# VectorE's order in an embedding tower on one Trainium2 core: the bias of a column step ahead of the scaling of the step before

## The reference, cut to what matters

```
x = layer_norm(dense_t @ Wd.T, gd, bd)
y = layer_norm(jnp.einsum('bnd,ed->bne', sparse_t, Ws), gs, bs)
y = jnp.einsum('bne,pn->bep', y, Wsi)
y = layer_norm(y, gsi, bsi)
y = jnp.swapaxes(y, 1, 2)
T = jnp.concatenate([x[:, None, :], y], axis=1)
Z = jnp.einsum('bnd,bmd->bnm', T, T)
out = layer_norm(Z[:, TRIL_I, TRIL_J] @ Wl.T, gl, bl)
h = jnp.concatenate([out * mask, r_dense_t], axis=1)
h = jnp.maximum(h @ W_top1 + b_top1, 0.0)
h = jnp.maximum(h @ W_top2 + b_top2, 0.0)
y = h @ W_top3
```

## Time and profile before

| what | value |
|---|---|
| runs of the kernel | 614.75, 616.3, 616.88 us |
| median | 616.3 us |
| span of the profiled execution, first to last instruction | 614.1 us |
| TensorE matmul busy | 526.2 us, 86% |
| VectorE busy | 499.9 us, 81% |
| GpSimd busy | 401.2 us, 65% |
| ScalarE busy | 339.1 us, 55% |

### The profile page before, as it was taken

One profiled execution on the slowest core, in us unless ns is written; L12 is line 12 of the kernel. 1 busy time (PEld: TensorE's weight loads), 2 busy tenths in 40 slices (PEclk: granted clock), 3 DMA queues, 4 the chain that ended last, 5 costly groups with the idle time before them and its releaser, 6 DMA issues.

```text
span 614.1 us, 17721 instructions
## 1 busy us (share of the span) xinstructions
PE 526.2 (86%) x6955; PEld 392.2 (64%) x6955; DVE 499.9 (81%) x977; ACT 339.1 (55%) x922; POOL 401.2 (65%) x422
## 2 busy tenths in 40 slices
PE   2458767789999998899999999999999998979877
PEld 1356546466766766576767676676767675756557
DVE  5597999979798989689898989898998988886510
ACT  3122536466675747375756566575747575755432
POOL 6777777777777777777777777777777777400000
PEclk9999889899999999899999999999999999999998
DMA  7311111111111111111111111112111111100000
GB/s 168 119 26 36 28 28 36 27 36 28 37 28 38 28 37 28 35 29 30 36 27 37 27 37 28 36 29 38 27 36 28 27 28 28 19 1 3 2 0 2
DMA packets 22611, 20.23 MB, mean 33 GB/s; under 512 B 12016, under 2 KB 14720, under 8 KB 22528
## 3 DMA queue, kind: packets, MB, share of 16 engines
q0 software_dynamic: 13312, 13.66, 12.5%
q1 hardware_dynamic: 8400, 4.33, 2.7%
q10 hardware_dynamic: 816, 1.11, 0.6%
HBM read 19.07 MB, written 0.01 MB: 31 GB/s over the span
## 4 chain that ended last, share of the span: by engine, by line
PE 38%; POOL 24%; issue 15%; DVE 10%; ACT 9%; DMA 4%; ACTq 0%; DVEq 0%; POOLq 0%
POOL emb L262 24%; PE b_l L404 7%; PE b_y L349 6%; PE b_l L421 6%; PE b_l L430 5%; PE b_z L361 5%; DMA emb<-in_tbl,idx 3%; ACT mixed L516 2%; DVE V L833 2%; DVE yb L815 2%; PE b_mix L337 2%; PE b_a L319 2%; DVE byn L810 2%; PE b_a L328 2%; DVE var_y L822 1%
## 5 line engine op out<-in xcount | busy, mean ns | idle before, releaser
L262 POOL DMA_INDIRECT emb<-in_tbl,idx x416 | 400.5, 963 | 128.2 <-issue 118.5
L521 ACT ACTIVATE sq<-yb 128x1024 f32<-128x1024 f32 x64 | 67.7, 1057 | 136.0 <-DVE yb L815 136.0
L815 DVE TENSOR_TENSOR yb<-b_y,bias_y 128x1024 f32<-128x1024 f32 x64 | 78.2, 1221 | 22.6 <-PE b_y L349 22.6
L349 PE MATMUL b_y<-mixed,projw 64*128 64x512 f32 x256 | 74.9, 663 | 23.5 <-ACT mixed L516 23.5
L833 DVE TENSOR_TENSOR V<-yb,rstd_y 128x256 f32<-128x256 f32 x256 | 91.9, 422 | 2.2
L822 DVE TENSOR_REDUCE var_y<-sq 128x32 f32<-128x1024 f32 x64 | 77.8, 1216 | 6.7 <-ACT sq L521 5.6
L404 PE MATMUL b_l<-wlt,zt 128*128 128x512 f32 x160 | 72.9, 602 | 0.8 <-issue 0.8
L328 PE MATMUL b_a<-gram_w,embt 128*128 128x128 f32 x416 | 67.1, 306 | 5.3 <-ACT embt L497 4.7
L337 PE MATMUL b_mix<-mix,byn 128*128 128x128 f32 x512 | 71.6, 285 | 0.0
L497 ACT ACTIVATE embt<-b_a 128x512 f32<-128x512 f32 (+1 forms) x64 | 33.0, 516 | 62.7 <-PE b_a L319 62.7
L337 PEld LDWEIGHTS b_mix<-mix,byn 128*128 128x128 f32 x512 | 65.5, 200 | 0.2
(11 more groups left out here) (132 smaller groups left out, 735.8 us busy)
## 6 DMA issues: line engine op xcount, KB each, us to landing
emb<-in_tbl,idx POOLq DMA_INDIRECT x416
dense<-in_r_dense_t SPq DMA_DIRECT2D x16, 128.0 KB, 2.1
V<-in_L_rec_Wl ACTq DMA_DIRECT2D x1, 1056.0 KB, 5.4
w<-in_W_top SPq DMA_DIRECT2D x2, 512.0 KB, 7.1
w<-in_W_top SPq DMA_DIRECT2D x1, 768.0 KB, 5.3
out_y<-y_sb SPq DMA_DIRECT2D x16, 0.5 KB
idx<-in_ids SPq DMA_DIRECT2D x1, 195.0 KB, 5.2
wd<-in_L_rec_Wd SPq DMA_DIRECT2D x1, 128.0 KB, 4.3
```

The costliest lines, as they stand in the source:

```text
L262: pool.indirect_dma_start(out=emb[t % 2][:, f, :], out_offset=None, in_=tables[f], in_offset=bass.IndirectOffsetOnAxis(ap=idx[:, t, f:f + ...
L349: last = nc.tensor.matmul(b_y[:, j2, :], projw[r, :], mixed[c % 2][r, :], start=True, stop=True, tile_position=(64 * j2, 0))
L815: nc.vector.tensor_tensor(yb[c % 2][:, :, :, :].rearrange("e h s p -> e (h s) p"), b_y[:, :, :].rearrange("e h (s p) -> e (h s) p", p=NP), ...
```

## The change

In VectorE's loop, `add_bias` of step `k` is called ahead of `scale` of step `k - 1`. Before, it was called behind `scale`, `recip_o` and `recip_x`. No instruction is added or removed, and the lists of the other engines are as they were.

```
                     normalize(t, 1)
                     shuffle(t)
+                if bc:
+                    add_bias(*bc)
                 if cc:
                     scale(*cc)
                 if (t := tile(h, INTERACT_NORM)) is not None:
                     recip_o(t)
                 if (t := tile(h, DENSE_NORM)) is not None:
                     recip_x(t)
-                if bc:
-                    add_bias(*bc)
                 if ab:
                     norms(*ab)
```

## The result

The changed kernel takes 720.3 us (median of 4 runs, 718.95 to 722.86) against 616.6 us before (median of 4, 614.75 to 617.34). The ratio is 1.169, with a 95% interval of 1.165 to 1.172. The forecast was 705 us with a range of 682 to 724 us: the direction came out, and the loss is 103.7 us instead of 88.6.

A forecast was written before the change was run, and what follows sets the result against it. The gathers set the pace at 33.0 us a tile, leaving compute about 0.5 us of room. Added waits of 70.4 us and 18.2 us of slow clock, together 88.6, on 616.3 us gave 705 us, range 682 to 724 us.

The forecast's parts named there:

- The wait for r_o: In c = 0 quarters, layer 2 waits for r_o behind the bias and starts 3.74 us after the projection: 3.62 us more.
- the Trainium skill's rule on long idle gaps: Long idle gaps between matmul bursts send TensorE's clock to half rate; cited against the clock holding (686.7 us, chance 0.17).
- The terms of c = 1 and of c = 2 with c = 3: Gram product waits for the later V, 0.25 us; scaling lengthens VectorE's chain through the last two quarters, 1.68 us a tile.
- The tile without the clock: A tile's 32.28 us plus 3.62, 0.25 and 1.68 us of added waits: 37.83 us, above the gathers' 33.0.
- The clock's price: TensorE's clock falls to half rate behind the new c = 0 wait, 14 times at 1.3 us: 18.2 us.
- a rival for all of them: The clock falls for twice as long behind each c = 0 wait: 14 x 2.6 = 36.4 us, 723 us, chance 0.08.
- The estimate by the Trainium skill's rule: Half the throttled time for 14 falls of 3.4 us on TensorE: 23.8 us, giving 710.5 us.
- The waits before the change: Four TensorE waits of 2.6 to 3.3 us in the earlier trace; the new 3.7 us wait was called longer than any.
- Steps 0 to 7 at nothing: The first eight steps have no r_o and waits for gathers hide the rest: 0 us, or 2 x 1.9 us uncovered.
- The quarter with c = 0 without r_o: With r_o's wait hidden, this quarter adds nothing; the tile grows only by 1.93 us, to 34.21 us.
- the rival of 636 us: The wait for r_o is hidden by something missed between projection and layer 2: tile 34.21 us, chance 0.05.
- The end: Behind step 60: one more r_o quarter 3.62 us, one c = 1 0.25, last variance 0.5, plus 1.3 for the clock.

The follow-up runs named there:

- The run with c = 2 alone: Against the kernel before the change, bias first only in the quarters with c = 2, from step 8 on: 629.2 us, 1.020 of before.

## Why the prediction was right, and where it fell short

*The wait for r_o* (3.62 us a tile) was right: layer 2 starts 3.83 us behind the projection, where 3.74 were forecast. It is shown by the runs that move r_o alone, with 66.4 us less in one direction and 12.7 us more in the other. That the Trainium skill's rule on long idle gaps would come true here ("TensorE: Matmul & The Clock Gate", section "Why this matters for your kernels") the trace confirms: each of the 14 waits has its fall to 0.50.

*The terms of c = 1 and of c = 2 with c = 3* (0.25 and 1.68 us) were right: 0.26 and 1.64 us in the tile that is shown. The run with c = 2 alone has the same 1.64 us in these two quarters. The tile without the clock (37.83 us) was measured as 37.65 us, in the run with 4 matmuls in the wait.

*The clock's price* is the first term that was mis-sized. The step took 1.3 us a fall, with 1.7 as the upper bound, because a fall lasted 3.4 us in all four cases before. Measured are 2.05 us a fall, some 1.45 us for a short one and 2.3 to 2.7 us for a long one. The price of a short fall was nearly right; the length was not. Ten of 14 falls lasted twice as long, which I had as a rival for all of them with a chance of 0.08. Sum: 28.7 us instead of 18.2. The estimate by the Trainium skill's rule, half the throttled time, has the same fault, as it too was worked out with 3.4 us; with the measured lengths, 10 x 6.8 + 4 x 3.4 = 81.6 us, half of which is 40.8, it is too high for what was measured. Part of a fall lies in the wait itself: that of 338.7 us begins 0.85 us before layer 2 starts, at 339.55 us. The waits before the change were also misread. The stretches of the earlier trace rows lie inside them; in TensorE's timeline the four are 3.85, 3.17, 2.75 and 2.73 us long, so the new one is not longer than any of them. The first, shown here, is as long:

```profile
81.34 1.12 PE L319 MATMUL b_a<-ident,emb 128*128 128x128 f32 x4 [3.85 <-DMA emb<-in_tbl,idx]
```

Its fall lasted 3.4 us all the same. Two more falls of before, at 105.1 and 600.0 us, stand behind waits of 1.75 and 2.01 us. So the length of the wait alone does not tell the length of the fall; what does stays open.

*Steps 0 to 7 at nothing* is the step that failed. I had named the cover, waits for gathers, and a price of 2 x 1.9 us without it. That price came from a tile in the middle of the span, where layers of other tiles stand between the projection and the gram product. In the first tiles they do not, and V's delay reaches TensorE directly: the tile of steps 4 to 7 takes 5.2 us longer than with the old order, not 1.9, with one fall of the clock among them. The first eight steps cost 9.0 us in the trace and 7.1 us in the run that leaves them alone.

*The quarter with c = 0 without r_o* was counted at nothing in the rival of 636 us. The run with r_o ahead shows that it costs 0.67 us a tile there, where the gram product waits 0.63 us for V. This changed nothing in the forecast, because r_o's wait covers it.

*The end* took 8.4 us instead of 5.7. It holds the quarter of step 60 with a long fall, and one more fall behind that than before (686.8 and 707.3 us, where there was one at 600.0); it was not taken apart further.

Together: 10 us of the 15 that were missing are the clock's, and 7 are the first steps'; by difference, the other terms were forecast some 2 us too high.

## What to carry to other kernels

An instruction list that is worked in order makes a wait common to all that stands behind the waiting instruction: before moving a waiting instruction up, look at what it now stands ahead of, down to the smallest ([128x1] here), and at who waits for that on the other engines. A delay is priced by the quarter in which it falls, so look at the first tiles apart, where the work that covers it in the middle is not yet there. A wait of TensorE costs itself and then the slow clock behind it, which here was half as much again (2.05 us on 3.8).

## What the runs showed of the hardware that I had not expected

- The stretches at 0.50 behind the waits for r_o (3.83 us at layer 2) come in two lengths, 3.4 and 6.8 us: 10 of 14 were long in the changed kernel, and 4 of 14 in the one with the bias first in c = 0 only. With r_o behind the norms, where 12 waits of layer 2 are 5.09 us, all 12 lasted 6.8 us. What sets the length was not found.
- Unused matmuls in a wait, 3.7 us of them in each tile, made the kernel 28.7 us faster than the same kernel with an idle TensorE.
- In the trace a float32 matmul is two records, each with 0.45 us at 512 columns. A transpose on TensorE is one: L319 has 208 records for 208 transposes. So only the counts of matmuls in the views have to be halved.
